# Mixing four streams with small diagonals on TensorE during the transpose, loads of x by tile, and the division at the end of VectorE's step

## The reference

```python
x = x + tanh(g_xattn) * attention(layernorm(x), ctx)
# then, for every row t of layernorm(x), cut into n = 4 streams of C = 512:
H_res  = sinkhorn_log(x_norm @ W_res.T + base)       # 50 iterations
H_pre  = softmax(x_norm @ W_pre.T + base)
H_post = softmax(x_norm @ W_post.T + base)
x_pre  = einsum('btnc,btn->btc', x_streams, H_pre)   # the branch's input
y      = x_pre @ W_branch
out    = einsum('btij,btjc->btic', H_res, x_streams) + einsum('btc,btn->btnc', y, H_post)
x = x + tanh(g_ffn) * out
```

## Time and profile before

| | us |
|---|---|
| median of 3 runs | 1848.66 (1835.97 to 1850.15) |
| the profiled execution, whole | 1840.6 |
| its span in the profile | 1838.5 |
| TensorE busy | 1372.7 (75%) |
| VectorE busy | 1341.3 (73%) |
| ScalarE busy | 1134.8 (62%) |
| POOL busy | 818.7 (45%) |
| mean granted TensorE clock | 0.903 |

### The profile page before, as it was taken

One profiled execution on the slowest core, in us unless ns is written; L12 is line 12 of the kernel. 1 busy time (PEld: TensorE's weight loads), 2 busy tenths in 40 slices (PEclk: granted clock), 3 DMA queues, 4 the chain that ended last, 5 costly groups with the idle time before them and its releaser, 6 DMA issues.

```text
span 1838.5 us, 35833 instructions
## 1 busy us (share of the span) xinstructions
PE 1372.7 (75%) x12448; PEld 838.8 (46%) x12448; DVE 1341.3 (73%) x3566; ACT 1134.8 (62%) x2273; POOL 818.7 (45%) x1373
## 2 busy tenths in 40 slices
PE   2778888988898888888888888888888886512223
PEld 0445555644555545555555545555555554301011
DVE  3333333555569887988788978988798878779987
ACT  3456777767667777777577757776777665311111
POOL 3223334344646564656555664656465634430000
PEclk9899999999989999999999999999999997755556
DMA  8456666655656655676666666676566554321122
GB/s 262 130 150 166 166 189 180 174 160 159 179 155 191 197 180 170 201 198 176 185 202 199 199 178 196 199 199 169 160 179 179 146 130 115 103 80 57 57 95 111
DMA packets 173923, 299.88 MB, mean 163 GB/s; under 512 B 23568, under 2 KB 74640, under 8 KB 169648
## 3 DMA queue, kind: packets, MB, share of 16 engines
q1 hardware_dynamic: 156336, 264.03, 45.4%
q0 software_dynamic: 17408, 33.56, 10.4%
HBM read 179.81 MB, written 67.11 MB: 134 GB/s over the span
## 4 chain that ended last, share of the span: by engine, by line
DVE 34%; ACT 15%; issue 15%; POOL 14%; PE 14%; DMA 6%; SPq 2%; POOLq 0%; ACTq 0%; DVEq 0%
POOL kp L556 6%; PE pr L655 6%; DVE ssum L1207 5%; DMA xc<-in_dram 4%; DVE otile_even L1236 4%; DVE otile_odd L1236 3%; ACT squares L918 3%; DVE xpre L1224 3%; DVE sa L1208 3%; DVE negm L1085 2%; DVE sv L1208 2%; POOL x1c L498 2%; DVE o_sb L1093 2%; DVE otile_even L1252 2%; ACT xt L910 2%
## 5 line engine op out<-in xcount | busy, mean ns | idle before, releaser
L1207 DVE TENSOR_REDUCE ssum<-kp 128x16 f32<-128x64 f32 x768 | 181.2, 236 | 122.6 <-POOL kp L556 118.1
L556 POOL TENSOR_TENSOR kp<-ke,sa 128x64 f32<-128x64 f32 x343 | 152.7, 445 | 244.1 <-DVE sa L1208 244.1
L769 PE MATMUL av_ps<-probs,v_t 128*32 128x128 f32 x2048 | 111.7, 289 | 188.5 <-DVE o_sb L1093 179.1
L556 POOL TENSOR_TENSOR kp<-ke,sv 128x64 f32<-128x64 f32 x329 | 149.1, 453 | 210.2 <-DVE sv L1208 209.5
L878 ACT ACTIVATE probs<-st_ps,key_bias 128x512 f32<-128x512 f32 x256 | 175.4, 685 | 97.0 <-PE st_ps L756 95.6
L1093 DVE TENSOR_TENSOR o_sb<-av_ps,rden 128x128 f32<-128x128 f32 x256 | 73.1, 285 | 212.5 <-ACT rden L887 208.2
L655 PE MATMUL pr<-x_hl,wq 128*128 128x512 bf16 x768 | 191.4, 403 | 36.2 <-POOL x_hl L479 36.2
L479 POOL TENSOR_TENSOR x_hl<-xc,x_hl 128x512 bf16<-128x512 f32 x128 | 151.4, 1183 | 117.3 <-ACT x_hl L846 117.1
L655 PE MATMUL pr<-x_hl,wk 128*128 128x512 bf16 x768 | 203.0, 421 | 0.0
L1085 DVE TENSOR_REDUCE negm<-s_ps 128x4 bf16<-128x512 f32 x256 | 166.1, 649 | 43.0 <-PE s_ps L742 42.8
L669 PE MATMUL pr<-wv,ctx_hl 128*128 128x256 bf16 x1536 | 181.9, 276 | 18.1 <-DVE k_hl L1070 15.0
(11 more groups left out here) (149 smaller groups left out, 3065.8 us busy)
## 6 DMA issues: line engine op xcount, KB each, us to landing
xs<-in_dram SPq DMA_DIRECT2D x128, 256.0 KB, 7.0
xc<-in_dram SPq DMA_DIRECT2D x32, 1024.0 KB, 7.6
ctx_raw<-in_dram SPq DMA_DIRECT2D x32, 1024.0 KB, 8.1
x1c<-in_dram POOLq DMA_DIRECT2D x64, 512.0 KB, 8.1
x_dram<-x1c SPq DMA_DIRECT2D x32, 1024.0 KB, 4.5
q_st<-q_hl SPq DMA_DIRECT2D x384, 64.0 KB
k_st<-k_hl SPq DMA_DIRECT2D x384, 64.0 KB
x1t_even<-x_dram SPq DMA_DIRECT2D x16, 1024.0 KB, 5.7
```

What stands on the lines that cost most here:

```text
L556: nc.gpsimd.tensor_tensor(kp[:], ke[:], v, ALU.mult).then_inc(kp_made, 1)
L769: nc.tensor.matmul(av_ps[rows, 0:W], v_t[:, G % 2, w, et * P + h * DH:et * P + (h + 1) * DH], probs[:, k % 2, h * W:(h + 1) * W], start=Tr ...
L1207: cf.link(nc.vector.tensor_reduce(s_t, k, AX.X, ALU.add))
```

## The change

The transpose of the branch's input becomes a matmul that mixes. For each tile ScalarE makes five 128 x 128 diagonals (the identity times pre_i for the four streams, and times the bias; `diagonals`), at -6. TensorE multiplies each block of 128 columns of the four streams, as the stationary operand, by its diagonal, and a block of ones by the fifth, all added up in PSUM: 5 matmuls for each of 4 blocks (`mix_pre`). Two blocks come at the end of the step before `pre`, two in it, and `pre` moves from -3 to -4 (r = 2 in place of 3) and ahead of the k projection in the order of the banks. xpre and VectorE's three products go. Further: x is loaded by tiles of 256 KB, each one step after the split of the tile before it in the same place; ctx_raw is loaded in r = 4; the division is the last thing in VectorE's step; and ScalarE's exp comes behind `norm_x` and `hi_x`.

```diff
@@ -54,6 +54,7 @@
 RING = 4
 
 HI_X_AT, LOW_X_AT = [1, 4, 5, 6], [3, 5, 6, 7]
+LOAD_X_AT = [n + 1 for n in LOW_X_AT]
 HI_CTX_AT, LOW_CTX_AT = [0, 0, 1, 1], [1, 2, 2, 3]
 
 T_AT, LOGITS_AT, SELECT_AT = [3, 3, 4, 4], 5, 9
@@ -68,9 +69,9 @@
 COEF_AT = SINK_AT + len(SINK)
 RETURN_AT = SINK_AT + SINK.index((RETURN, None))
 
-BESIDE = dict(load=-8, first=-6, xpre=-5, pre=-3, branch_0=0, branch_1=1, out_0=-1, out_1=0,
+BESIDE = dict(load=-8, diag=-6, pre=-4, branch_0=0, branch_1=1, out_0=-1, out_1=0,
               stream_1=0, stream_2=1, y=2, stream_3=4, pair_1=5, pair_2=6, pair_3=7, store_0=5, store_1=8)
-BEHIND = dict(load=-5, first=-3, xpre=-3, pre=-2, branch_0=-1, branch_1=-1, out_0=-1, out_1=0,
+BEHIND = dict(load=-5, diag=-3, pre=-2, branch_0=-1, branch_1=-1, out_0=-1, out_1=0,
               stream_1=0, stream_2=1, y=2, stream_3=3, pair_1=3, pair_2=4, pair_3=5, store_0=4, store_1=6)
 LAST_BESIDE = B - 3
 TILE_AT = {(f, t): UNITS * (f + 1) + 54 + UPC * t for f in range(LAST_BESIDE + 1) for t in range(DT)}
@@ -130,6 +131,8 @@
 
     G, r = chunk_step(g)
     made = [("sel", f, 0) for f in ffn_at(g, UPC + SELECT_AT)]
+    made += [("pre", f, t) for f, t in tiles_at(g, "pre")]
+    assert len(made) < 2
     if 0 <= G + 1 < NG:
         made += {0: [("q", G + 1, 0)], 1: [("q", G + 1, 1)], 2: [("k", G + 1, 0)], 3: [("k", G + 1, 1)],
                  4: [("v", G + 1, 0)], 7: [("v", G + 1, 1)]}.get(r, [])
@@ -137,7 +140,6 @@
         made += [("o", G - 1, 2 * (r - 5)), ("o", G - 1, 2 * (r - 5) + 1)]
     made += [("t", H, j) for H, j in at_step(g, 2, T_AT)]
     made += [("lg", H, 0) for H, j in at_step(g, 2, [LOGITS_AT])]
-    made += [("pre", f, t) for f, t in tiles_at(g, "pre")]
     if g == -1:
         made.append(("csum", 0, 0))
     return made
@@ -254,7 +256,8 @@
         post = sb("post", [P, 3, DT, N])
         xt = sb("xt", [P, LG, 512])
         lgs = sb("lgs", [P, NC, 512])
-        xpre = sb("xpre", [P, C])
+
+        diag = sb("diag", [P, N + 1, P])
         xpt = sb("xpt", [P, C])
         otile = [sb("otile_even", [P, N, C]), sb("otile_odd", [P, N, C])]
 
@@ -278,7 +281,7 @@
         ffn_loaded = sem("ffn_loaded")
         xs_loaded = [sem(f"xs_loaded{i}") for i in range(XSN)]
         xs_taken = sem("xs_taken")
-        xc_loaded = sem("xc_loaded")
+        xc_loaded = [sem(f"xc_loaded{i}") for i in range(DT)]
         ctx_loaded = sem("ctx_loaded")
         mask_loaded = [sem(f"mask_loaded{i}") for i in range(NC)]
         masks_loaded = sem("masks_loaded")
@@ -333,8 +336,7 @@
         lg_copied = sem("lg_copied")
         small_req = sem("small_req")
         small_done = sem("small_done")
-        xp_first = sem("xp_first")
-        xpre_ready = sem("xpre_ready")
+        diag_made = sem("diag_made")
         y_full = sem("y_full")
         y_read = sem("y_read")
         pre_ready = sem("pre_ready")
@@ -370,8 +372,11 @@
 
         @block.sync
         def _(sp):
-            def load_xc(G):
-                sp.dma_start(xc[:], xr[G // NC, :, :, cols(G)]).then_inc(xc_loaded, 16)
+            def load_xc(G, t):
+
+                if G:
+                    sp.wait_ge(x_split, DT * (G - 1) + t + 1)
+                sp.dma_start(xc[:, t, :], xr[G // NC, :, t, cols(G)]).then_inc(xc_loaded[t], 16)
 
             def load_ctx(G):
                 sp.dma_start(ctx_raw[:], cr[G // NC, :, :, cols(G)]).then_inc(ctx_loaded, 16)
@@ -424,7 +429,8 @@
                 load_xs(0, p)
             for dst, src in SMALL_LOADS:
                 sp.dma_start(dst, src).then_inc(small_loaded, 16)
-            load_xc(0)
+            for t in range(DT):
+                load_xc(0, t)
             for G in range(NC - 1):
                 load_mask(G)
             sp.dma_start(maskt, mask_t.rearrange("b p n -> p b n")).then_inc(masks_loaded, 16)
@@ -438,9 +444,9 @@
             for g in range(FIRST, LAST):
                 G, r = chunk_step(g)
                 b, u = divmod(g, UNITS)
-                if r == 0 and 1 <= G + 2 < NG:
-                    sp.wait_ge(x_split, DT * (G + 2))
-                    load_xc(G + 2)
+                for H, t in at_step(g, -2, LOAD_X_AT):
+                    if H + 1 < NG:
+                        load_xc(H + 1, t)
                 if r == 2 and 0 <= G - 2 < NG:
                     store_x1(G - 2)
                 for later in STAT_PIECES.get(g + 4, []):
@@ -457,7 +463,7 @@
                         sp.wait_ge(negrow_ready, 1)
                     sp.dma_start(k_st[ROWS:ROWS + 1, (G + 1) % 2].rearrange("p t h j -> p (t h) j"),
                                  bcast(neg_rows[G + 1:G + 2, :], 1, HEADS)).then_inc(stack_loaded[(G + 1) % 2], 16)
-                if r == 6 and 1 <= G + 2 < NG:
+                if r == 4 and 1 <= G + 2 < NG:
                     sp.wait_ge(ctx_split, G + 2)
                     load_ctx(G + 2)
                 if r == 7 and NC <= G + 4 and G + 3 < NG:
@@ -722,12 +728,21 @@
                 if part:
                     ins.then_inc(bank_full, 1)
 
-            def transpose_pre(what):
+            def mix_pre(what, part):
+
                 kind, f, t = what
-                pe.wait_ge(xpre_ready, DT * f + t + 1)
-                for j in range(C // P):
-                    ins = nc.tensor.transpose(bank(what)[:, j * P:(j + 1) * P], xpre[:, j * P:(j + 1) * P], id_sb[:])
-                ins.then_inc(bank_full, 1)
+                n = DT * f + t
+                if part == 0:
+                    pe.wait_ge(x1t_loaded[n % 2], 16 * (n // 2 + 1))
+                    pe.wait_ge(diag_made, n + 1)
+                for j in (2 * part, 2 * part + 1):
+                    block = bank(what)[:, j * P:(j + 1) * P]
+                    for i in range(N):
+                        at = i * C + j * P
+                        nc.tensor.matmul(block, x1t[n % 2][:, at:at + P], diag[:, i, :], start=(i == 0), stop=False)
+                    ins = nc.tensor.matmul(block, ones[:], diag[:, N, :], start=False, stop=True)
+                if part:
+                    ins.then_inc(bank_full, 1)
 
             def scores(k):
                 G, w, et = place(k)
@@ -793,7 +808,7 @@
                     values(g - 2)
                 made = banked_at(g)
                 for n, what in enumerate(made):
-                    if what[0] != "sel":
+                    if what[0] not in ("sel", "pre"):
                         bank_free(what)
                     if what[0] in "qk":
                         project_x(what)
@@ -808,7 +823,7 @@
                     elif what[0] == "sel":
                         select(what, 1)
                     elif what[0] == "pre":
-                        transpose_pre(what)
+                        mix_pre(what, 1)
                     else:
                         sum_w(what)
 
@@ -819,9 +834,13 @@
                 for part in range(2):
                     for f, t in tiles_at(g, f"branch_{part}"):
                         branch(f, t, part)
-                for f in ffn_at(g, UPC + SELECT_AT - 1):
-                    bank_free(("sel", f, 0))
-                    select(("sel", f, 0), 0)
+                for what in banked_at(g + 1):
+                    if what[0] == "sel":
+                        bank_free(what)
+                        select(what, 0)
+                    elif what[0] == "pre":
+                        bank_free(what)
+                        mix_pre(what, 0)
 
         @block.scalar
         def _(act):
@@ -833,8 +852,8 @@
                 nc.scalar.activation(ctx_hl[:, 0, t, :], ctx_raw[:, t, :], ACT.Copy).then_inc(ctx_hi, 1)
 
             def norm_x(G, t):
+                act.wait_ge(xc_loaded[t], 16 * (G + 1))
                 if t == 0:
-                    act.wait_ge(xc_loaded, 16 * (G + 1))
                     act.wait_ge(xstat_ready, G // NC + 1)
                 nc.scalar.activation(xc[:, t, :], xc[:, t, :], ACT.Identity, bias=ra[:, 4, t:t + 1],
                                      scale=ra[:, 2, t:t + 1]).then_inc(x_norm, 1)
@@ -947,16 +966,16 @@
                     ins = nc.scalar.activation(sln[:], sv[:].rearrange("p t i -> p (t i)"), ACT.Ln)
                 ins.then_inc(small_done, 1)
 
-            def first_products(f, t):
-                n = DT * f + t
-                act.wait_ge(x1t_loaded[n % 2], 16 * (n // 2 + 1))
+            def diagonals(f, t):
                 if t == 0:
                     act.wait_ge(pre_ready, f + 1)
-                if n:
-                    f0, t0 = divmod(n - 1, DT)
+                if f or t:
+                    f0, t0 = divmod(DT * f + t - 1, DT)
                     act.wait_ge(bank_full, PLACE["pre", f0, t0] + 1)
-                nc.scalar.activation(xpre[:], x1t[n % 2][:, 0:C], ACT.Identity, bias=rb[:, f % 3, 6, t:t + 1],
-                                     scale=pre[:, f % 3, t, 0:1]).then_inc(xp_first, 1)
+                for i in range(N):
+                    nc.scalar.activation(diag[:, i, :], id_sb[:], ACT.Identity, scale=pre[:, f % 3, t, i:i + 1])
```

(31 more changed lines are left out.)

## The result

The changed kernel takes 1867.34 us (median of 4 runs, 1866.77 to 1867.94), the kernel before 1849.41 (1835.97 to 1852.95): a ratio of 1.0125, 95% interval 1.0088 to 1.0163. It is slower by 1.25%, where the prediction had 1840, faster by half a per cent. The time lies in the stated range, on the wrong side of no change. The profiled executions stand further apart, 1865.8 us of span against 1838.5: +27.3 us, where the sum of the prediction was -8.5.

What follows compares the result with a forecast made beforehand. No engine bound alone: VectorE full in r = 0 to 2, ScalarE setting the pace in r = 2 to 5. Terms -27+32+10-1.5-11-3-8 gave -8.5 to -9 against 1840.6: 1832 profiled, median 1840, range 1808 to 1876.

Steps and rivals of the forecast that it cites:

- Loads by tile: Start and chunks 1 to 9: earlier loads of xc remove ScalarE's waits and slow projections, 27 us saved of a possible 33.
- The pace of the mix: TensorE, end of r = 1 and head of r = 2: each half of 20 instructions takes 2.2 us, bounds 2.1 to 4.3.
- The dear matmul: Rival, TensorE's mix: load and matmul take turns, a half takes 4.3 us, +88 us, 1928 us; chance 0.05.
- The way to gelu: Chunks 10 to 26: halves ahead of the key projection make gelu 3.4 us late, about 1.5 us lost a chunk.
- The division last: VectorE, r = 6 and 7: division no longer covers POOL's answer time, 0.2 us each, 0.4 us a chunk.
- The rival by which every half-iteration is laid open: The fourth half-iteration waits for kp in all steps: 1.8 us more for 20 chunks, +36, 1876 us; chance 0.15.
- The chunks with a selection: Among chunks 10 to 26: priced like the others, 1.5 us plus 0.4 for the division, 9.5 us for the five.
- Chunks 27 to 31: Shorter steps, rden binds sooner: 2.8 us more each for 27 to 29, 1.5 for 30; chunk 31 gains 1.5.
- The tail: After the last chunk: fewer VectorE products and TensorE mixing early save 11, 3 and 8 us.
- the 1.0 to 1.5 of the estimate: ScalarE, r = 0: the five small 128x128 products take 1.0 to 1.5 us a tile, costed at nothing.

Runs made afterwards that it cites:

- The mix alone: The kernel before with only TensorE's mix added (loads, exp and division as before): 1882.19 us, ratio 1.0203.
- the key first: The changed kernel with the first key projected before the second half of the mix, the mixed tile copied a step later: 1815.51 us, ratio 0.9860.
- the cut mix: The changed kernel with two of the mix's five matmuls left in every block, output wrong, a probe only: 1804.22 us, ratio 0.9770.
- the last kernel: The kernel with the mix early plus selection ahead of `values`, chunk 31's copy a step later, SP's loads behind the stacks for g < 0: 1769.36 us.
- The selection ahead of `values`: The changed kernel with the selection's second half moved ahead of `values` in u = 17, once in four chunks: 1846.63 us, ratio 1.0023.
- the kernel with the mix early: The changed kernel with key projected first, division in its old place, and the mix's first half ahead of `values` in r = 1: 1779.61 us, ratio 0.9650.
- the run with exp in its old place: The kernel with the mix early, with ScalarE's exp back ahead of the normalisation of x: 1780.37 us, ratio 0.9649.
- SP's order altered: The kernel with the mix early, with SP's loads of x behind the stacks of their step and ctx loaded in r = 6: 1781.76 us.
- the loads alone: The kernel before with only x loaded by tile and ctx loaded in r = 4: 1818.84 us, ratio 0.9875.

## Why the prediction was wrong

**Loads by tile: right, but for the start.** -27 forecast, -24.2 measured with what the start costs. Chunks 2 to 5 are 37.4 us (37 to 38 forecast), the waits of the earlier trace rows are gone but for one, and so are the slow projections of the earlier trace rows. The one is the first, at 46 us: the prediction took its 3.0 us as gained, and ScalarE waits 3.49 there now. What was too small is the price of SP's queue: 1 us charged, 2.5 us at the first `maximum` and 2.0 more in chunk 0. The step said that behind the waits stood "stores and the stacks, all with steps of slack outside chunks 0 and 1"; inside them there is none, and the rows of SP's timeline above show it.

**The pace of the mix: right.** 2.2 us a half forecast. Here a half begins at 1045.65, and the transposed scores behind it at 1047.94: 2.3 us. The dear matmul is refuted. The four fp32 matmuls of a block are 8 instructions, two each, in 1.06 to 1.11 us. The 8 instructions in 1.04 us of the earlier trace rows are 8 transposes by the identity, one each. So a matmul of a 128 x 128 block takes about twice the 0.11 us of a transpose: 0.22 us.

The Trainium skill, TensorE: Matmul & The Clock Gate, Terms, gives the transpose mode as four times faster for fp32. By that a matmul would have taken four times what a transpose does; the trace shows twice.

**The way to gelu: right.** Forecast 12.8 us after the division of r = 0 and r = 3 ending 19.3 us after the start of r = 1; measured 13.1 and 19.5. (Two slips in its working change nothing: 5.56 - 1.53 is 4.03 and not 3.96, and the three waits of the earlier trace rows stand in TensorE's own r = 1, 2 and 3, while VectorE is in r = 0, 1 and 2.) The twelve chunks without a selection cost 25.6 us where 22.8 was forecast. The mix alone, the key first and the cut mix show the cause: the two halves ahead of the key projection.

**The division last: there where forecast, and cancelled elsewhere.** Forecast +0.4 us a chunk, laid open in r = 6 and 7. These are there (0.23 and 0.24 us), and 0.2 in r = 2. But behind a late rden the new place saves 0.4 to 0.9 us in r = 3, so in the plain chunks of the changed kernel it is worth nothing; on the kernel before, where rden is on time, it costs 0.7 to 0.8 a plain chunk in the mean and 20 us in all, after the 10 that the early chunks gain. The rival by which every half-iteration is laid open (1.8 us more a chunk) is refuted.

**The chunks with a selection: the step that failed.** The prediction says "In the chunks with a softmax it is 1.5 as well", adds 0.4 for the division, and prices them from the chain of gelu alone: 9.5 us for the five. They cost 25.8. Chunk 10 costs 1.5, and that agreement is luck in part: in u = 17 and 18 the kernel before ran at the low clock there (6.8 us of it) and the changed one at the high. The four others cost 5.5 to 7.2 each. `values` of r = 1 waits 1.76 to 1.89 us for the division in them (0.19 or nothing before), the clock falls to 1.2 GHz between 0.3 us before that wait ends and 1.5 us after, and just these steps have no cover: the selection and the query projection stand between that wait and the read that POOL and VectorE wait for.

In the kernel before, the low clock fell in u = 16 and u = 19 (3.4 us in each, chunks 14 to 26), and there it costs nothing: u = 16 takes 7.6 us at either level, and u = 19 of chunk 18 takes 6.64 us at the low level in the kernel before and 6.64 at the high one in the last kernel. The prediction had used the clock for the early chunks and for the tail and had left it out for the middle, where the windows of the earlier trace rows show a mean of 0.96 too: some 7 us of low clock in a chunk with a selection. It moved. The selection ahead of `values` shows it: no low clock is left in these chunks, and they are 5.0 to 6.7 us shorter, 15.6 us of it the clock by the estimate above. Without these 15.6 us the change would still have been slower by some 12 us of span, where the forecast was faster by 8.5; the next largest part of that is chunks 27 to 31.

**Chunks 27 to 31: too small.** Forecast 2.8 us for 27 to 29 and 1.5 for 30; measured 3.6, 3.4, 5.5 and 4.5. r = 3 is 9.4 to 9.8 us there too, but was 4.9 to 6.1 before. In r = 1 VectorE gives back only 1.2 in chunks 27 and 28 (5.63 to 4.41), where there are no statistics. The clock has a part here as well: the kernel before had no low clock in chunks 27 to 30, the changed one has 3.4 us of it in three of them and 10.2 in chunk 29, where r = 1 is at the low clock and gives back 0.1. Chunk 31 was given -1.5 because it "has no projections", and takes 2.1 more. ScalarE's timeline there, 1564 to 1574:

```profile
1566.72 0.60 ACT L985 ACTIVATE xpt<-pr 128x512 f32<-128x512 f32 x1 [1.78 <-PE pr L743]
1567.34 1.28 ACT L910 ACT_TABLE_LOAD   x1
```

Gelu needs no projection here, and stands behind the copy of the mixed tile, which waits for the mix. The copy was in r = 3, behind gelu, before the change; that the change moves it to r = 2 was counted as a relief ("left ScalarE's crowded r = 3") and not as a wait put ahead of gelu. With the copy a step later chunk 31 is 34.1 us, against 35.9 and 37.3 in two kernels with the same program there and the copy in r = 2; the 1.4 us between these two go with the clock, which is low under the mix in the one and high in the other. r = 3 is 4.55 us in it, as it was before the change.

**The tail: nearly right.** -22 forecast, -18.9 measured. The part up to the copy of the fourth tile from the end is 11.7 us shorter (225.6 to 213.9 us after the last `maximum`), and from there to the end 7.2 (69.2 to 62.0); forecast were 14 and 8. The prediction lets TensorE mix "as soon as x1t has landed". It doesn't always. For the tile that landed at 1806.4:

```profile
1813.84 2.93 ACT L996 ACTIVATE otile_even<-x1t_even,ccon,cmat 128x512 f32<-128x512 f32 x4 [9.40 <-POOL cmat L583]
1816.68 1.26 ACT L976 ACTIVATE diag<-id_sb,pre 128x128 f32<-128x128 f32 x4
1817.85 0.39 ACT L977 ACTIVATE diag<-id_sb,rb 128x128 f32<-128x128 f32 x1
1818.35 1.78 PEld L742 LDWEIGHTS pr<-diag,x1t_odd 128*128 128x128 f32 x8 [10.98 <-issue]
1818.38 2.05 PE L742 MATMUL pr<-diag,x1t_odd 128*128 128x128 f32 x8 [10.18 <-ACT diag L977]
```

The diagonals stand behind the first output products of the tile before, which wait 9.40 us for the matrices of the batch, and TensorE waits 10 us for them. VectorE hardly pays for that, since it waits 0.22 us for the branch of this tile. It pays at the next one, whose mix waits 3.44 us for its load and whose copy stands ahead of the first output products on ScalarE:

```profile
1839.99 2.91 DVE L1244 SCALAR_TENSOR_TENSOR otile_even<-x1t_even,cmat,otile_even 128x512 f32<-128x512 f32 x4 [2.39 <-ACT otile_even L996]
```

The diagonals take 1.56 us a tile (1816.68 to 1818.24), slightly over the 1.0 to 1.5 of the estimate.

**The exp.** The prediction left the new place of exp out. It is worth nothing in the kernel with the mix early, by the run with exp in its old place; in the changed kernel itself it was not tried.

What stays open: why the changed kernel's median is 18 us over that of before and its profiled execution 27. The kernel before ran at 1835.97 to 1856.21 us in these sessions, and 1840.6 is near the low end; the changed one lies within 1.2 us. Why the one scatters and the other doesn't was not tried.

## What to carry to other kernels

Work that is moved to an engine with idle time helps only if it lands in that idle time: look at what stands on each side of the wait. TensorE had 5 us of waits in three steps, all ahead of `values`, and the halves were put behind it, ahead of the one projection that ScalarE's longest chain waits for; the same 4.4 us, one half ahead of `values` and the other behind the projection (with the division back), turned +1.25% into -3.5%. When work is added ahead of a chain, list everything that queues behind it on each engine (here the copy of the mixed tile too), and count the clock among the things that move: a filled wait was worth 5.0 to 6.7 us a chunk here, where the work that fills it gave 1.7 in a chunk at the high clock. And time the parts of a compound change one by one, since the loads alone would have been a gain of 1.25%.

## What the runs showed of the hardware

Three things were not expected.

TensorE's clock fell to 1.2 GHz at the end of a wait of only 1.76 us: u = 17 of chunk 18 in the changed kernel, after a wait of 1.72 us in the step before, at which it had stayed at 2.4. In chunks 14 and 26 it fell 1.5 us after the end of one of 1.89 us. With the second wait filled it did not fall there.

Where it falls depends on when the stretch begins. The kernels with the mix early and with SP's order altered differ in SP's queue alone; chunks 14, 18, 22, 26 are 51.8, 48.4, 51.7, 48.5 us in the one and 48.5, 51.7, 48.4, 51.8 in the other, which begins chunk 14 3.0 us later. Within each of them the four chunks have one program. That is 3.3 us a chunk for nothing but its place in time. In the short ones the low clock comes in u = 16 and TensorE then waits 0.3 us or not at all ahead of `values` in u = 17; in the long ones it is at the high clock in u = 16, waits 1.76 to 1.88 us in u = 17, and the low clock follows there.

The Trainium skill, TensorE: Matmul & The Clock Gate, Part 1, says that activity is judged in a window that runs freely and isn't reset by the kernel; the trace agrees with a phase that the program doesn't set.

An edit can so bring the low clock into chunks that it doesn't touch (6 and 30 in the last kernel, 3.2 and 3.1 us), and a difference of a few us between two kernels isn't shown to be that of the edit until the granted clock of the two stretches has been compared.
